# Relative scores of a causal attention, stored as one row of 1280 per head from four buffers

## The reference, cut to what matters

```python
Er_s = Er[start:, :]                                   # 512 x 16
QEr = jnp.einsum('bhsd,ld->bhsl', q, Er_s)             # relative scores
Srel = _skew(QEr)                                      # row p shifted left by 511 - p
QK = jnp.einsum('bhsd,bhtd->bhst', q, k)
attn = (QK + Srel) / math.sqrt(dh)
causal = jnp.tril(jnp.ones((S, S), dtype=bool))
attn = jnp.where(causal[None, None], attn, -jnp.inf)
attn = jax.nn.softmax(attn, axis=-1)
out = jnp.einsum('bhst,bhtd->bhsd', attn, v)
```

## Time and profile before

| | |
|---|---|
| median of three runs | 7131.78 us |
| the profiled execution, its own time | 7131.68 us |
| its span in the trace | 7130.0 us |
| stretch of `rel_scores` from the first copy to the first load of `causal_attention` | 195.4 to 584.4 us |
| stretch of `causal_attention` | 584.4 to about 1235 us |
| busy share of PE, DVE, ACT, POOL over the span | 69%, 56%, 39%, 27% |
| DMA packets, bytes over the span | 503550, 679.98 MB |

### The profile page before, as it was taken

The page is one execution under the profiler, slowest core; times in us unless marked ns, Lnnn a source line. Parts: engine busy times, 40 slices in busy tenths (PEclk is TensorE's granted clock), DMA queues, the critical chain, the costliest instruction groups (busy, mean ns, idle before and its releaser), DMA issues. The chain is left out here.

```text
span 7130.0 us, 108835 instructions
## 1 busy us (share of the span) xinstructions
PE 4954.3 (69%) x25218; PEld 2892.3 (41%) x25218; DVE 4005.8 (56%) x8286; ACT 2764.5 (39%) x5926; POOL 1940.0 (27%) x2979
## 2 busy tenths in 40 slices
PE   6344666492777873996667476767767696885897
PEld 3112333240442332882312264556655483222543
DVE  6223555537546765442656696644966455785464
ACT  2223555015225632221234255632555431662252
POOL 0002443000025620220022255411554123451242
PEclk9556888695888986998878798988989897998697
DMA  4888996100052321110466133110332005231543
GB/s 148 224 243 202 190 187 160 44 0 0 0 174 77 89 51 42 41 42 25 133 122 116 40 121 112 60 32 24 109 119 78 28 11 187 77 82 47 165 120 90
DMA packets 503550, 679.98 MB, mean 95 GB/s; under 512 B 102218, under 2 KB 323052, under 8 KB 503105
## 3 DMA queue, kind: packets, MB, share of 16 engines
q1 hardware_dynamic: 437384, 504.19, 24.4%
q0 software_dynamic: 65792, 171.82, 10.7%
HBM read 402.70 MB, written 254.56 MB: 92 GB/s over the span
## 5 line engine op out<-in xcount | busy, mean ns | idle before, releaser
L1110 DVE TENSOR_REDUCE t_nmax<-t_aps 128x2 f32<-128x1024 f32 x700 | 851.4, 1223 | 366.4 <-PE t_aps L1037 352.3
L1215 ACT ACTIVATE t_expT<-t_bps 128x512 f32<-128x512 f32 x1290 | 672.9, 601 | 295.9 <-PE t_bps L1056 267.7
L1056 PE MATMUL t_bps<-t_Q,t_K 51*128 51x512 f32 (+2 forms) x1290 | 462.7, 476 | 127.8 <-ACT t_expT L1215 103.4
L1037 PE MATMUL t_aps<-t_K,t_Q 49*128 49x512 f32 (+2 forms) x1400 | 422.8, 449 | 63.1 <-DMA t_K<-k_halves 28.5
L2386 DVE TENSOR_TENSOR f_hl<-f_h,f_hh 128x512 fp32r<-128x512 f32 x192 | 203.9, 1062 | 423.2 <-ACT f_hh L2317 423.2
L1086 PE MATMUL t_ops<-t_expT,t_V 128*17 128x512 f32 (+1 forms) x2560 | 408.8, 606 | 0.0
L3711 ACT ACTIVATE t_relsb<-t_relsb,t_nmax 128x128 f32<-128x128 f32 (+3 forms) x515 | 279.5, 560 | 311.3 <-DVE t_nmax L3684 307.3
L1056 PEld LDWEIGHTS t_bps<-t_Q,t_K 51*128 51x128 f32 (+2 forms) x1290 | 185.2, 188 | 521.5 <-ACT t_expT L1215 394.4
L3645 PE MATMUL t_tps<-ident,t_relsb 128*128 128x128 f32 x1280 | 261.6, 312 | 173.4 <-ACT t_expT L3530 165.9
L3359 ACT ACTIVATE t_prob<-t_summed,t_nmax 128x256 f32<-128x256 f32 (+1 forms) x552 | 261.1, 474 | 303.7 <-DVE t_nmax L3410 303.7
L2674 POOL TENSOR_TENSOR a_crossed<-a_qsb,a_tab 128x256 f32<-128x256 f32 x272 | 263.5, 991 | 308.3 <-ACT a_qsb L2620 279.1
(11 more groups left out here) (419 smaller groups left out, 12618.8 us busy)
## 6 DMA issues: line engine op xcount, KB each, us to landing
rel<-r_out SPq DMA_DIRECT2D x128, 256.0 KB, 2.1
t_relsb<-rel SPq DMA_DIRECT2D x128, 256.0 KB, 5.0
t_Q<-q_halves POOLq DMA_DIRECT2D x420, 64.0 KB, 2.6
t_K<-k_halves POOLq DMA_DIRECT2D x420, 64.0 KB, 2.6
rel<-r_out SPq DMA_DIRECT2D x128, 192.0 KB, 1.9
t_relsb<-rel SPq DMA_DIRECT2D x128, 192.0 KB, 3.6
k_halves<-a_parts SPq DMA_DIRECT2D x48, 512.0 KB
q_halves<-a_parts SPq DMA_DIRECT2D x48, 512.0 KB, 5.4
```

Of the source, the lines that this page charges most:

```text
L1037: last = nc.tensor.matmul(aps[:, (t * PPG + i) % 2, x, :], operand(Qr, KA, p, h, slice(t * P, (t + 1) * P)), operand(Kr, KA, p, h, slice(0 ...
L1056: nc.tensor.matmul(bps[:, slot_of(kb, j), :], operand(Kr, KB, p, h, slice(kb * P, (kb + 1) * P)), operand(Qr, KB, p, h, slice(0, S)), star ...
L1110: nc.vector.tensor_reduce(nmax[:, g, t, i * HPT:(i + 1) * HPT], aps[:, (t * PPG + i) % 2], AX.X, ALU.max, negate=True).then_inc(s["maxed"], 1)
L1215: nc.scalar.activation(expT[:, kb % RING, j, :], bps[:, slot_of(kb, j), :], ACT.Exp).then_inc(s["expo"], 1 + (PAD if end else 0))
```

## The change

`out` has four buffers in place of two, each with its own semaphore (`st0` to `st3`). The four tiles of a head, which already stood side by side in `out`, are stored by one DMA as one row of 1280 f32 (5120 bytes) per partition. `rel` is one DRAM tensor of 128 heads by 128 rows by 1280 in place of four. The skewed loads stay four per head, with the same rows of 512 to 2048 bytes, but step by 1279 elements. The copies of the first four heads wait for no store and stand ahead of the loops of DVE and ACT, which run over four heads at a time. PE's two PSUM halves stay.

```diff
+    RING = 4
+    W = 10 * P
-        out = sb("out", [P, 2, 10 * P])
+        out = sb("out", [P, RING, W])
...
-                with sp.Fori(0, NB * H // 2) as i:
-                    for hp in range(2):
-                        n = i * 2 + hp
+                with sp.Fori(0, NB * H // RING) as i:
+                    for r in range(RING):
+                        n = i * RING + r
                         sp.wait_ge(s["cp_a"], n * 2 + 2)
+                        alone(sp)
                         sp.wait_ge(s["cp_v"], n * 2 + 2)
                         alone(sp)
-                        for t in range(NT):
-                            w = (t + 1) * P
-                            sp.dma_start(rel[t][ds(n, 1), :].rearrange("o (p c) -> (o p) c", c=w),
-                                         out[:, hp, OFF[t]:OFF[t] + w]).then_inc(s[f"st{hp}"], 16)
+                        sp.dma_start(rel[ds(n, 1), :].rearrange("o (p c) -> (o p) c", c=W), out[:, r, :]).then_inc(s[f"st{r}"], 16)
...
-                        dve.wait_ge(s[f"st{hp}"], i * (16 * NT) + 16 * NT)
+                        if not first:
+                            alone(dve)
+                            dve.wait_ge(s[f"st{r}"], i * 16)
...
-                            nc.vector.tensor_copy(out[:, hp, OFF[t]:OFF[t] + w], o[:, hp * NT + t, 0:w]).then_inc(s["cp_v"], 1)
+                            nc.vector.tensor_copy(out[:, r, OFF[t]:OFF[t] + w], o[:, r % 2 * NT + t, 0:w]).then_inc(s["cp_v"], 1)
...
+                copies(0, True)
+                with dve.Fori(0, NB * H // RING - 1) as i:
+                    copies(i + 1)
...
-                        row = rel[t][ds(n, 1), P - 1:]
-                        skewed = bass.AP(row.tensor, row.offset, [[w - 1, P], [1, w]])
+                        row = rel[ds(n, 1), OFF[t] + P - 1:]
+                        skewed = bass.AP(row.tensor, row.offset, [[sum(WIDTH) - 1, P], [1, w]])
...
-            rel = [dram(f"rel{t}", [NB * 16, P * (t + 1) * P]) for t in range(NT)]
+            rel = dram("rel", [NB * 16, P * 10 * P])
```

More of the change, by code:

```diff
@@ L1239, in rel_scores @@
     KR = 6 * DH
-    with phase(nc, name, "er cast erp q0 q1 q_free mm mm_free_a mm_free_v cp_a cp_v st0 st1 dvc") as (s, sb, ps):
+    RING = 4
+    W = 10 * P
+    with phase(nc, name, "er cast erp q0 q1 q_free mm mm_free_a mm_free_v cp_a cp_v st0 st1 st2 st3 dvc") as (s, sb, ps):
         er32 = sb("er32", [KR, S])
@@ L1268, in _ @@
             def _(sp):
-                for hp in range(2):
-                    sp.sem_inc(s[f"st{hp}"], 16 * NT)
-                with sp.Fori(0, NB * H // 2) as i:
-                    for hp in range(2):
-                        n = i * 2 + hp
+                with sp.Fori(0, NB * H // RING) as i:
+                    for r in range(RING):
+                        n = i * RING + r
                         sp.wait_ge(s["cp_a"], n * 2 + 2)
+                        alone(sp)
                         sp.wait_ge(s["cp_v"], n * 2 + 2)
                         alone(sp)
-                        for t in range(NT):
-                            w = (t + 1) * P
-                            sp.dma_start(rel[t][ds(n, 1), :].rearrange("o (p c) -> (o p) c", c=w),
-                                         out[:, hp, OFF[t]:OFF[t] + w]).then_inc(s[f"st{hp}"], 16)
-                for hp in range(2):
-                    sp.wait_ge(s[f"st{hp}"], 16 * NT + 16 * NT * NB * H // 2)
+                        sp.dma_start(rel[ds(n, 1), :].rearrange("o (p c) -> (o p) c", c=W), out[:, r, :]).then_inc(s[f"st{r}"], 16)
+                for r in range(RING):
+                    sp.wait_ge(s[f"st{r}"], 16 * NB * H // RING)
             @block.tensor
@@ L1317, in _, with copies @@
                 dve.sem_inc(s["mm_free_v"], 2)
-                with dve.Fori(0, NB * H // 2) as i:
-                    for hp in range(2):
-                        n = i * 2 + hp
+                def copies(i, first=False):
+                    for r in range(RING):
+                        n = i * RING + r
                         dve.wait_ge(s["mm"], n + 1)
-                        dve.wait_ge(s[f"st{hp}"], i * (16 * NT) + 16 * NT)
+                        if not first:
+                            alone(dve)
+                            dve.wait_ge(s[f"st{r}"], i * 16)
                         for t in (0, 3):
                             w = (t + 1) * P
-                            nc.vector.tensor_copy(out[:, hp, OFF[t]:OFF[t] + w], o[:, hp * NT + t, 0:w]).then_inc(s["cp_v"], 1)
+                            nc.vector.tensor_copy(out[:, r, OFF[t]:OFF[t] + w], o[:, r % 2 * NT + t, 0:w]).then_inc(s["cp_v"], 1)
                         dve.wait_ge(s["cp_v"], n * 2 + 2)
                         dve.sem_inc(s["mm_free_v"], 1)
+                copies(0, True)
+                with dve.Fori(0, NB * H // RING - 1) as i:
+                    copies(i + 1)
             @block.scalar
@@ L1332, in _, with copies @@
                 act.sem_inc(s["mm_free_a"], 2)
-                with act.Fori(0, NB * H // 2) as i:
-                    for hp in range(2):
-                        n = i * 2 + hp
+                def copies(i, first=False):
+                    for r in range(RING):
+                        n = i * RING + r
                         act.wait_ge(s["mm"], n + 1)
-                        act.wait_ge(s[f"st{hp}"], i * (16 * NT) + 16 * NT)
+                        if not first:
+                            alone(act)
+                            act.wait_ge(s[f"st{r}"], i * 16)
                         for t in (1, 2):
                             w = (t + 1) * P
-                            nc.scalar.copy(out[:, hp, OFF[t]:OFF[t] + w], o[:, hp * NT + t, 0:w]).then_inc(s["cp_a"], 1)
+                            nc.scalar.copy(out[:, r, OFF[t]:OFF[t] + w], o[:, r % 2 * NT + t, 0:w]).then_inc(s["cp_a"], 1)
                         act.wait_ge(s["cp_a"], n * 2 + 2)
                         act.sem_inc(s["mm_free_a"], 1)
+                copies(0, True)
+                with act.Fori(0, NB * H // RING - 1) as i:
+                    copies(i + 1)
 def outproj(nc, G, name, src, w, shape, bias, gate, onto, also=None, tile_k=None, sums=None, H=16):
```

## The result

The changed kernel has a median of 7014.91 us (7001.74 to 7024.93, six runs) against 7134.93 us before (7130.37 to 7140.3, six runs). The ratio is 0.983 with a 95% interval of 0.9817 to 0.9842: 120 us, 1.7% faster. The prediction was 7015 us with a range of 6996 to 7054.

The account below looks back on a forecast made before the run. Latency and too few buffers held steady stretches; afterwards the DMA engines would bind. Start 203.0, loads 84, 113 heads x 1.58 = 178.5 and landing 2.3 gave 467.8 against 584.4 us: 7131.8 - 116.6 = 7015 us, range 6996 to 7054.

Parts of the forecast that it names:

- Two kinds of stretch, neither bound by an engine: Phase of the change, before: steady stretches held by latency and too few buffers, 2.39 us a head; stores waiting behind query loads.
- The price of a row: DMA engines, steady stores: 9 ns a packet plus 36.7 ns per 1000 bytes, so a head goes from 2.39 to 1.58 us.
- The ring no longer binds with four buffers: Store buffers: one comes round in 3.2 to 4.9 us, so four allow 0.8 to 1.2 us a head, under 1.58.
- SP has time: SP's store queue: one store issued a head, where four took 1.88 us, so issue does not bind.
- The loads: Six query loads in the phase: 14.0 us each, 84 us together, with 2.5 heads getting through beside each, 15 in all.
- The landing and the barrier: End of the phase: 2.3 us for the last store's landing and the barrier before the next phase.
- The sum: Start of the next phase: 203.0 + 84 + 178.5 + 2.3 gives 467.8 us instead of 584.4, a gain of 116.6 us.
- a cap of the stores near 360 GB/s: Rival, steady stores: longer rows save nothing, 1.83 us a head, gain 88 us, time 7043; chance 0.12.
- 278 GB/s: Rival, steady stores: writes into `rel` themselves are slow, 2.36 us a head, gain 28 us, time 7103; chance 0.05.
- Slower reads: Rival, phase reading `rel` back: spread rows slow skewed reads; 32% slower (117 us) cancels the gain, far bound 7315; chance 0.02.
- loads and stores get along better: Rival, beside query loads: 5.6 heads a load and 1.50 us a head, gain 154 us, time 6978; chance 0.05.
- the half-way case: Beside query loads: half of the better-sharing rival, 4 heads a load at 1.50 us, time 6995, the range's low end.

## Why the prediction was right, point by point

- *Two kinds of stretch, neither bound by an engine*: shown. Without the later loads the phase is 317.5 us: 128 heads at 2.39 us are 306, and the wait at the start is some 11 more.
- *The price of a row*: it gave 1.58 us a head at full share. It was solved from two stretches, and a third bears it out: 1270 packets at 9 ns and 5.79 MB at 36.7 ns per 1000 bytes are 223.9 us, and 16 engines at a share of 1.006 over 14 us spent 225.3. DVE's pace is 1.64, 3% more than 655,360 bytes at 414 GB/s. The number of buffers is not the cause, since eight leave it at 1.64. In the 26.2 us in which DVE starts 16 heads (429.21 to 455.41) the engines move 2365 packets, which is 16.4 heads. So the engines together are ahead of the landings that free the buffers, as they would be if some of the 16 finish their part of a store later than others; that is not shown, and the cause of the gap stays open. It put 7 us on the sum.
- *The ring no longer binds with four buffers*: right, and with two it binds at 2.05 us. An undisturbed store of 640 KB lands in 3.0 us, in the middle of my bounds of 2.1 and 3.7. In the change it is 5.4, above both, since the full engines make a store queue; the bounds had left that out, and it cost nothing.
- *SP has time*: right for one store a head. That SP would be the bound with four buffers and four stores was expected at 2.1 to 2.2 us and was 2.34.
- *The loads*: this term was mis-sized. I took 14 us with 2.5 heads beside, which is a price of 14 - 2.5 x 1.58 = 10 us a load. Measured are 7.6, or 3.9 heads beside each load. Six times 2.4 us are 14 us too much in the sum.
- *The landing and the barrier*, 2.3 us: with the measured terms the sum is 203 + 6 x 7.6 + 128 x 1.637 = 458.1, and the next phase starts at 462.6. The 4.5 us left over are these two, and whatever the start costs beyond 203 us.
- *The sum*: the next phase was forecast at 467.8 us and stands at 462.6. The errors are -14, +7 and +2 us and partly cancel. The total met the forecast to 0.1 us, which is luck: the gain in the phase is 5 us larger, and later phases drift by more than that from run to run.
- *Two sums of the rivals are slightly off*: 94 heads at 1.50 give 430.3, not 430.7, which leaves the time at 6978; and 4 heads a load at 1.50 give 203 + 84 + 104 x 1.50 + 2.3 = 445.3 and a time of 6993, not 6995, so the low end of the range should have been 6993. Neither matters for the outcome.
- *The rivals*: a cap of the stores near 360 GB/s is excluded by 414 GB/s, 278 GB/s too. Slower reads are excluded by the layout alone, to within some 8 us. That loads and stores get along better than I took was partly so: 3.9 heads beside a load, close to the 4 of the half-way case, but at 1.64 us a head and not at 1.50.

## What to carry to other kernels

When a loop of stores leaves the DMA engines a quarter idle, write down three numbers for an item, namely packets and bytes at their price, the landing time with the copy divided by the number of buffers, and the issuing queue's time, and expect a gain only down to the second largest. Here more buffers alone gave 40 us, one store of long rows alone 53, and both 122. Buffers have a second use, which the pace of a steady stretch does not show: after each interruption, here the loads of queries, they let the engines run full for a while, and that was most of the 40 us. Look also at how many neighbouring partitions a DMA writes: spreading the same 16 over all 96 partitions of the operand, in both phases, was worth another 93 us; the matmul sums over the partitions, so their order is free to choose.

## What the runs showed of the hardware

- How much stores get beside dense loads depends on the length of their rows. In the earlier trace rows they got 0.81 MB in 14 us with rows of 512 to 2048 bytes. In the change, in a like stretch (329 to 343 us), they got 2.22 MB with rows of 5120 bytes, in fewer packets (488 against 804):

```profile
q1 hardware_dynamic: 488, 2.22, 54.4%
q0 software_dynamic: 461, 1.53, 47.5%
```

The number of buffers differs there too. With the four buffers of the change and rows of 512 bytes (281 to 295 us) they got 0.68 MB, so the length of the rows matters most; waiting stores add to it, as the run with eight buffers showed:

```profile
q0 software_dynamic: 472, 1.57, 77.8%
q1 hardware_dynamic: 1360, 0.68, 28.9%
```

- A packet is one row for SP's stores, but not for POOL's loads: a load of 256 KB in rows of 1024 bytes is 80 packets (2880 for 36 loads, 225 to 430 us of the change), of which 16 are semaphore writes, so that a packet carries 4096 bytes.
- While two batches of loads stood in q0 at the start, q1 moved nothing at all for 6.5 us, before and after. Why it is shut out there and not in the later loads is not settled.
- The share of the DMA engines tells that they are occupied, not that they work: at the start it is 105% at 112 GB/s with neighbouring partitions, and 104.3% at 209 GB/s with spread ones.
- A busy share can be full although the work is cheap to others: the loads of a batch (1.573 MB, 14 us alone at 112 GB/s and full share) cost the stores beside them only 7.6 us.
